# Three small attentions in a transformer stack: two tiles side by side in rounds, or one tile after the other on every engine

## The reference, cut to what matters

```python
x = x + _L0_attn_ref(_layernorm(x, axis=-1), ...)
Q = (X @ Wq.T + bq).reshape(B, S, H, d_head) * scale      # H = 16 heads of 16
K = (X @ Wk.T + bk).reshape(B, S, H, d_head) * scale
V = (X @ Wv.T + bv).reshape(B, S, H, d_head)
scores = jnp.einsum('bqhd,bkhd->bhqk', Q, K)              # causal mask, then softmax
out = jnp.einsum('bhqk,bhkd->bqhd', attn, V).reshape(B, S, D)
return out @ Wo.T + bo
```

## Time and profile before

| | |
|---|---|
| median of 3 runs | 3392.66 us (3380.62 to 3396.48) |
| the profiled execution's own time | 3396.48 us |
| its span in the profile | 3394.7 us |
| attention 1, in the span | 18.2 to 223.1 us |
| attention 2 | 229.8 to 441.5 us |
| attention 3 | 2537.4 to 2742.0 us |
| mean granted clock of TensorE | 0.928 of full speed |

### The profile page before, as it was taken

One profiled execution on the slowest core, in us unless ns is written; L12 is line 12 of the kernel. 1 busy time (PEld: TensorE's weight loads), 2 busy tenths in 40 slices (PEclk: granted clock), 3 DMA queues, 4 the chain that ended last, 5 costly groups with the idle time before them and its releaser, 6 DMA issues. The chain is left out here.

```text
span 3394.7 us, 49700 instructions
## 1 busy us (share of the span) xinstructions
PE 2916.8 (86%) x17527; PEld 1787.8 (53%) x17528; DVE 1579.7 (47%) x2705; ACT 1260.5 (37%) x2514; POOL 1232.9 (36%) x656
## 2 busy tenths in 40 slices
PE   5867734659999999999999999999977789999998
PEld 3544422535545554555455554555434467777776
DVE  3444567533554455444544464445526643333232
ACT  3433412114344334433443344344424333333332
POOL 0000000035676567656765676557650000000000
PEclk9778866679999999999999999999988899999999
DMA  1000030011111011110111111111011000000000
GB/s 40 0 17 0 0 121 0 0 58 40 36 49 39 25 35 49 39 35 33 41 39 35 39 35 39 35 39 35 30 72 77 0 1 0 0 0 0 0 0 25
DMA packets 26434, 98.27 MB, mean 29 GB/s; under 512 B 3536, under 2 KB 8272, under 8 KB 24976
## 3 DMA queue, kind: packets, MB, share of 16 engines
q1 hardware_dynamic: 24720, 94.02, 8.4%
q10 hardware_dynamic: 1664, 3.58, 0.3%
HBM read 55.97 MB, written 2.10 MB: 17 GB/s over the span
## 5 line engine op out<-in xcount | busy, mean ns | idle before, releaser
L685 POOL TENSOR_TENSOR cx_acc<-cx_acc,cx_prob 128x1024 f32<-128x1024 f32 (+1 forms) x352 | 834.7, 2371 | 509.0 <-ACT cx_prob L965 501.5
L965 ACT ACTIVATE cx_prob<-cx_st 128x512 f32<-128x512 f32 (+1 forms) x832 | 477.5, 596 | 595.2 <-PE cx_st L814 577.5
L1062 DVE TENSOR_REDUCE cx_mhalf<-cx_mx 128x1 f32<-128x804 f32 x512 | 486.1, 988 | 219.2 <-PE cx_mx L790 219.1
L825 PE MATMUL cx_av<-cx_prob,cx_kv 128*64 128x512 f32 (+1 forms) x1664 | 456.8, 628 | 0.0
L813 PE MATMUL cx_st<-cx_q,cx_k 128*128 128x512 f32 (+1 forms) x832 | 369.0, 444 | 50.0 <-ACT cx_prob L965 49.4
L1528 PE MATMUL moe_gu<-moe_wgu,moe_xnT 128*128 128x352 f32 x1280 | 397.6, 462 | 0.0
L790 PE MATMUL cx_mx<-cx_kp,cx_q 128*128 128x402 f32 x1024 | 304.0, 380 | 62.6 <-DVE cx_mhalf L1062 59.2
L814 PE MATMUL cx_st<-cx_q,cx_k 128*128 128x512 f32 (+1 forms) x832 | 332.4, 400 | 0.0
L1528 PEld LDWEIGHTS moe_gu<-moe_wgu,moe_xnT 128*128 128x128 f32 x1280 | 241.5, 191 | 124.1 <-issue 6.2
L790 PEld LDWEIGHTS cx_mx<-cx_kp,cx_q 128*128 128x128 f32 x1024 | 174.7, 193 | 248.5 <-DVE cx_mhalf L1062 186.0
L1043 DVE TENSOR_TENSOR cx_turn<-cx_mx,cx_tab 128x384 f32<-128x384 f32 x256 | 130.9, 553 | 358.3 <-PE cx_mx L747 358.3
(11 more groups left out here) (209 smaller groups left out, 3701.3 us busy)
## 6 DMA issues: line engine op xcount, KB each, us to landing
cx_k<-cx_kp SPq DMA_DIRECT2D x32, 804.0 KB, 4.0
cx_ctx<-in_cx_ctxN SPq DMA_DIRECT2D x32, 416.0 KB, 3.2
cx_ctxr<-in_cx_ctxrN SPq DMA_DIRECT2D x32, 416.0 KB, 3.9
cx_k<-cx_kp SPq DMA_DIRECT2D x32, 402.0 KB, 5.2
moe_wgu<-in_moe_wgu SPq DMA_DIRECT2D x5, 1408.0 KB, 14.6
moe_wd<-in_moe_wd SPq DMA_DIRECT2D x4, 896.0 KB, 24.6
x_all<-in_x SPq DMA_DIRECT2D x1, 2048.0 KB, 4.2
cx_wq<-in_cx_wq SPq DMA_DIRECT2D x1, 2048.0 KB, 11.8
```

The source lines that it names most:

```text
L685: pool.tensor_tensor(acc[rows, :, :], sofar, prob[slot(kt)][rows, :, :], ALU.add).then_inc(s_acc, 1)
L825: last = pe.matmul(av[DCX * p:DCX * p + DCX, :], kv[e][0:nk(kt), kt, :], prob[slot(kt)][0:nk(kt), p, :], start=(kt == 0), stop=(kt == NKT ...
L965: act.activation(prob[slot(kt)][rows, p, :], st[p][rows, :], ACT.Exp).then_inc(s_exp, 1)
L1062: dve.tensor_reduce(mhalf[:, i // 2, i % 2:i % 2 + 1], mx[i % 2][:, :, 0:KQ], AX.XY, ALU.max)\
```

## The change

`rounds` goes out, for these three attentions, for `staggered`: the loop body treats one tile at a time, and each stage in it is given with the number of tiles by which it is ahead. `SLOTS`, the buffers and the six rounds in the loop (the last two are written out) stay at two tiles. In attentions 1 and 2 queries and keys are projected with the weights as the stationary side and `xnT` as the moving one, so that they come out transposed: `turn_qk`, `qk` and `keep_qk`'s old form go, and matmuls of 256 or 512 columns become twice or four times as many of 128. ScalarE adds the biases of attention 2 when it keeps `qT` and `kbd`. In all three, keys are transposed in `front`, not in `v`.

```diff
+def staggered(engine, first, body, start=lambda r: None):
+    def at(r, g, ahead):
+        return r + (g + ahead) // SLOTS, (g + ahead) % SLOTS
+    for stage, tile in first:
+        stage(*at(0, 0, tile))
+    with engine.Fori(0, ROUNDS - 2) as r:
+        start(r)
+        for g in range(SLOTS):
+            for stage, ahead in body:
+                stage(*at(r, g, ahead))
...
             def turn_x(r, g):
-                pe.wait_ge(s_xn, r * SLOTS + before + g + 1)
+                pe.wait_ge(s_xn, upto(r, g))
+                if not is_first(r):
+
+                    pe.wait_ge(s_kbd, upto(r - 1, g))
...
+                elif kind == "bias":
+                    for o in range(2 * DC):
+                        for c in range(DC):
+                            last = pe.matmul(front[g][:, o * P:(o + 1) * P], w["qk"][:, c, o * P:(o + 1) * P],
+                                             xnT[g][:, c, :], start=(c == 0), stop=(c == DC - 1))
...
             def scores(r, g):
 
-                pe.wait_ge(s_x, LEAD + r * SLOTS + before)
-                pe.wait_ge(s_qTc, r * SLOTS + before + g + 1)
-                pe.wait_ge(s_kbd, r * SLOTS + before + g + 1)
+                pe.wait_ge(s_x, two_before(r, g))
+                pe.wait_ge(s_kbd, upto(r, g))
...
-            rounds(pe, (turn_x, project, turn_qk),
-                   ((scores, 0), (turn_x, 1), (turn_probs, 0), (project, 1), (values, 0), (turn_qk, 1), (out, 0)))
+            if kind == "rope":
...
+                          ((turn_probs, 0), (turn_x, 3), (scores, 1), (values, 0), (turn_qk, 2), (project_qk, 3),
+                           (project_v, 2), (out, 0)))
+            else:
...
+                          ((turn_probs, 0), (turn_x, 2), (scores, 1), (values, 0), (project_qk, 2), (project_v, 2),
+                           (out, 0)))
...
+                    for c in range(DC):
+                        act.activation(qT[g][:, c, :], front[g][:, c * P:(c + 1) * P], ACT.Identity,
+                                       bias=w["bq"][:, c:c + 1])
+                    for c in range(DC):
+                        for i in range(4):
+                            last = act.activation(kbd[g][:, c, i, :], front[g][:, D + c * P:D + (c + 1) * P],
+                                                  ACT.Identity, bias=bk4[:, c, i:i + 1], scale=head4[:, i:i + 1])
...
+                staggered(act, ((keep_xT, 0), (keep_xT, 1), (keep_qk, 0), (keep_v, 0), (keep_qk, 1), (keep_v, 1),
+                                (exps, 0)),
+                          ((keep_probT, 0), (keep_xT, 2), (exps, 1), (keep_qk, 2), (keep_v, 2)))
...
+                          ((gather, 4), (shift, 1), (normalise, 4), (scale_heads, 0), (turn, 3), (update_x, 0)),
+                          start)
+            else:
...
+                          ((gather, 3), (shift, 1), (normalise, 3), (scale_heads, 0), (update_x, 0)),
+                          start)
```

More of the change, by code:

```diff
@@ L74, in rounds @@
                 stage(ROUNDS - 1, g)
+def staggered(engine, first, body, start=lambda r: None):
[8 more added lines that the diff above has]
+                stage(*at(r, g, ahead))
+    start(ROUNDS - 2)
+    for r in range(ROUNDS - 2, ROUNDS):
+        for g in range(SLOTS):
+            for stage, ahead in body:
+                if r * SLOTS + g + ahead < NT:
+                    stage(*at(r, g, ahead))
 def small_attention(nc, sb, pb, sem, kind, name, w, x_all, const, nth, steps_before):
@@ L143, in small_attention, with upto, two_before @@
     s_dve = sem("attention_dve_step")
-    steps_ahead = 2 + SLOTS * {"context": 0, "bias": 0, "rope": 1}[kind]
-    dve_steps = 2 + SLOTS * {"context": 2, "bias": 2, "rope": 3}[kind]
+    F = 3 if kind == "rope" else 2
+    tile_steps = 5 if kind == "rope" else 4
+    steps_ahead = 2 * (F + 1) + (F if kind == "rope" else 0) + 1
     def is_first(r):
         return isinstance(r, int) and r == 0
+    def upto(r, g):
+        return r * SLOTS + before + g + 1
+    def two_before(r, g):
+        return LEAD + r * SLOTS + before + g - 1
     with nc.Block() as block:
@@ L187, in turn_x, with project_qk @@
                 last.then_inc(s_xT, 1)
-            def project(r, g):
-                pe.wait_ge(s_xTc, r * SLOTS + before + g + 1)
-                if kind == "context":
-                    pe.wait_ge(s_ctx, r * SLOTS + before + g + 1)
-                    for c in range(DC):
-                        pe.matmul(front[g][:, 0:D], xnT[g][:, c, :], w["q"][:, c, :],
-                                  start=(c == 0), stop=(c == DC - 1))
-                    last = pe.matmul(front[g][:, D:2 * D], ctxT[g][:, :], w["k"][:, :], start=True, stop=True)
-                else:
+            def project_qk(r, g):
+                pe.wait_ge(s_xTc, upto(r, g))
+                if kind == "rope":
                     for c in range(DC):
@@ L253, in values @@
             def values(r, g):
-                pe.wait_ge(s_pTc, r * SLOTS + before + g + 1)
+                pe.wait_ge(s_pTc, upto(r, g))
                 for c in range(DC):
@@ L267, in out @@
             def out(r, g):
-                pe.wait_ge(s_on, r * SLOTS + before + g + 1)
+                pe.wait_ge(s_on, upto(r, g))
                 for c in range(DC):
@@ L351, in keep_qk, with gather @@
[L351 to L365 removed]
+            def gather(r, g):
+                x = x_all[:, bass.ds(r * SLOTS + g, 1), :]
+                step.done(dve.bn_stats(stats[g][:, :], x))
+                dve.memset(mv[0][:, 2:3], 0.0)
+                step.done(dve.bn_aggr(mv[g][:, 0:2], stats[g][:, :]))
+                dve.tensor_scalar(mv[g][:, 1:2], mv[g][:, 1:2], EPS, None, ALU.add).then_inc(s_var, 1)
@@ new lines, in normalise, with turn @@
+            def normalise(r, g):
+                x = x_all[:, bass.ds(r * SLOTS + g, 1), :]
+                dve.wait_ge(s_rstd, upto(r, g))
+                if not is_first(r):
+                    dve.wait_ge(s_xT, upto(r - 1, g))
+                dve.tensor_scalar(xn[g][:, :], x, mv[g][:, 0:1], rstd[g][:, 0:1], ALU.subtract, ALU.mult)\
+                    .then_inc(s_xn, 1)
+            def turn(r, g):
+                dve.wait_ge(s_qk, LEAD + upto(r, g))
+                t2p = t2[g][:, :].rearrange("p (n e) -> p n e", e=2)
+                fp = front[g][:, :].rearrange("p (n e) -> p n e", e=2)
+                sn = w["sin"][:, :].rearrange("p (n e) -> p n e", e=2)
+                dve.tensor_tensor(t1[g][:, :], front[g][:, :], w["cos"][:, :], ALU.mult)
+                dve.tensor_tensor(t2p[:, :, 0], fp[:, :, 1], sn[:, :, 0], ALU.mult)
+                step.done(dve.tensor_tensor(t2p[:, :, 1], fp[:, :, 0], sn[:, :, 1], ALU.mult))
+                dve.tensor_tensor(qk[g][:, :], t1[g][:, :], t2[g][:, :], ALU.add).then_inc(s_qkc, 1)
@@ L387, in start @@
             def start(r):
-                step.start(r * dve_steps + steps_before + steps_ahead)
+                step.start(r * SLOTS * tile_steps + steps_before + steps_ahead)
             step.start(steps_before)
-            rounds(dve, (normalise, keep_qk),
-                   ((normalise, 1), (shift, 0), (keep_qk, 1), (scale_heads, 0), (update_x, 0)), start)
-    return steps_before + ROUNDS * dve_steps
+            if kind == "rope":
+                staggered(dve, ((gather, 0), (gather, 1), (normalise, 0), (normalise, 1), (gather, 2), (normalise, 2),
+                                (turn, 0), (turn, 1), (turn, 2), (gather, 3), (normalise, 3), (shift, 0)),
+                          ((gather, 4), (shift, 1), (normalise, 4), (scale_heads, 0), (turn, 3), (update_x, 0)),
+                          start)
+            else:
+                staggered(dve, ((gather, 0), (gather, 1), (normalise, 0), (normalise, 1), (gather, 2), (normalise, 2),
+                                (shift, 0)),
+                          ((gather, 3), (shift, 1), (normalise, 3), (scale_heads, 0), (update_x, 0)),
+                          start)
+    return steps_before + NT * tile_steps
 CH, CK, CQ = 16, 128, 192
```

128 lines of the change are left out of this document (57 added, 71 removed).

## The result

The changed kernel takes 3291.05 us, the median of 4 runs (3290.18 to 3293.69); the kernel before, beside it, 3388.9 (4 runs, 3380.62 to 3396.48). The ratio is 0.9713, 95% interval 0.9687 to 0.9739: 2.9% faster, with the forecast of 3292 beside it. That agreement is partly luck: the total is right to 1 us, but between first and last scores one stage is 5.7 us worse than forecast and the two others together 7.2 us better. The profiled execution has a span of 3288.6 us, against 3394.7 for the one taken of the kernel before.

What follows compares the result with a forecast made beforehand. No engine was full: both tiles sat in softmax together, idling TensorE. Staggered steps of 8.9 to 9.2 us, with clock falls in attention 1, save about 105 us from 3396.48, giving 3292 us; range 3265 to 3345.

Steps and rivals of the forecast that it cites:

- The sum: Three attention stages take 148.3, 133.8 and 139.8 us, saving 104.4; with starts and tails about 105 us, giving 3292.
- The small terms: First scores about 3 us sooner in attention 1, 2 in attention 2, 3.7 later in 3; tails plus 0.3 each.
- a third tile's projection: Start of attention 3: a third tile is projected first, so the first scores come 3.7 us later.
- The cycle: VectorE's chain from `scores` to `scores`: 8.9 us a tile in attentions 1 and 2, 9.2 in 3, where `update_x` decides.
- my sum: TensorE's own work per tile in attention 2, from scores, transposes, values, projections and `out`: 7.6 us.
- the 4.8 of the range's end: Attention 2's 16 projection matmuls: 1.8 us, or 4.8 if new weights were not hidden behind a column stream.
- TensorE's 8.1 us in attention 3: TensorE's own work per tile in attention 3, which keeps `turn_qk` (four transposes, 0.46 us): 8.1 us.
- Rival C: All three attentions: gain lost in issue, six waits per tile costing 2.2 us a tile; 3392, chance 0.08 with what lies between.
- Rival D: All three attentions: slower, TensorE at 1.2 GHz with its work doubled to 13.9, 15.2 and 16.2 us; 3500, chance 0.05.
- hidden below 8.9 either way: ScalarE in attention 2: 6.0 us a tile, at most 8.2, covered because `values` can be 2 us late.
- The clock in attention 1: A 2.0 us wait for `out` drops TensorE's clock in about every second tile, making steps 9.9 us.
- Rival B: Clock swings in all three attentions from short waits, one fall of 2.0 us in every tile; 3357, chance 0.20.

Runs made afterwards that it cites:

- run 3: Changed kernel plus four more 128-column ScalarE activations a tile in attention 2 and one more VectorE rotation product in attention 3: 3320.34 us.
- run 9: Changed kernel with attention 1's context and its key and value weights padded with zeros from 64 to 128 rows: 3284.36 us.
- run 2: Changed kernel with attention 1's values made twice on TensorE and attention 2's `xn` made two more times on VectorE, into scratch: 3294.94 us.
- run 7: Changed kernel with `xn` made early, right behind its statistics and ahead of `shift`, in all three attentions: 3279.16 us.
- run 1: Changed kernel with `xn` made later, behind `scale_heads` in attentions 1 and 2 and behind `update_x` in attention 3: 3288.26 us.
- run 6: Changed kernel with attention 1's first 128 query columns projected twice and attention 2's query and key biases left out (five ScalarE instructions, not ten): 3285.15 us.
- run 10: Changed kernel with attention 1's context zero-padded, `xn` early in all three, and attention 2's key bias left out (four 256-column spreads): 3255.36 us.
- run 8: Kernel before with the stagger alone, queries and keys of attentions 1 and 2 still transposed, POOL's power ahead of the context copy: 3305.71 us against 3392.58.
- run 5: Kernel before, in rounds of two tiles, with only the turned projections of attentions 1 and 2 and biases on ScalarE: 3371.04 us against 3391.96.

## Why the prediction was right, and where it wasn't

**The sum.** Between first and last scores the three stages save 19.9, 47.7 and 38.1 us, 105.7 in all, where 104.4 was forecast. The first scores of attention 1 come 3.1 us sooner (forecast 3), those of attention 2 1.9 sooner counted from attention 1's last (forecast 2), those of attention 3 2.7 later (forecast 3.7), and what follows attention 3's last scores takes 2.0 us more. Together: 105.7 + 3.1 + 1.9 - 2.7 - 2.0 = 106.0; the two spans differ by 106.1. Each stage is within 6 us of its forecast: 154.0 for 148.3, 130.3 for 133.8, 136.1 for 139.8.

The small terms came out by luck. In run 3 attention 1 has the code of the changed kernel, and its first scores come at 27.4 us, not 30.3, because TensorE was at the lower clock for less of the start-up. The second tile's query matmuls, in the changed kernel and then in run 3:

```profile
26.14 2.07 PE L234 MATMUL a_front<-a_xnT,a_wq 128*128 128x128 f32 x8
...
25.06 1.16 PE L236 MATMUL a_front<-a_xnT,a_wq 128*128 128x128 f32 x8
```

In run 9, whose attention 2 has the changed kernel's code, its first scores come 40.0 us behind attention 1's last ones, where it was 38.5 and 40.4 before. And the way from attention 2's last scores to attention 3's first takes 2128.7 to 2135.7 us in the ten staggered kernels, so that its 2.7 us say little of a third tile's projection.

**The cycle: right.** 8.73 against 8.9 in attention 2 and 9.0 against 9.2 in attention 3. The waits for `out` were 1.72, 0.99 and 0.70 us against 2.0, 1.3 and 0.8, each a little shorter. In attention 2 TensorE's own work is 0.2 us longer than my sum: the 16 matmuls of the turned projection took 1.99 us (277.25 to 279.24) where I had 1.8, far from the 4.8 of the range's end. (TensorE's 8.1 us in attention 3 add up to 8.0 from my own terms; nothing hangs on it.) The stretches are 183, 164 and 171 us for 176, 166 and 174. The granted clock of "above 0.95" in attentions 2 and 3 was missed over the whole stretches (0.92 and 0.94) and met between first and last scores (0.99 and 0.97). The nature of the chain was tested from both sides: 0.65 us more on VectorE made attention 2 0.65 slower (run 2), one product more made attention 3 0.33 slower (run 3), and `xn` moved off the chain made attention 3 0.25 faster (run 7). Rival C is out, by attention 2 from its first to its last scores (busy time, then the waits):

```profile
222.90:353.20 130.30, 112.66 (x1597) 86.94 (x1596) 85.21 (x137) 92.86 (x237) 16.59 (x26) 0.99 0.00 1
```

```profile
PE a_score L303 <- DVE a_headsT L427: 13.6, 14, 1.0
```

Of 130.3 us TensorE is busy 112.7 and waits 13.6 for `headsT`; all else, issue included, is 4.0 us, 0.3 a tile. Rival D is out: in the steps of attention 1 TensorE at the lower clock got the full one back after 3.4 us each time.

**ScalarE: the step that failed, at no cost.** I said ScalarE is "hidden below 8.9 either way: what covers it is that `values` can be 2 us late". Two things are wrong in it. The ten activations of 128 columns take 3.4 us (279.82 to 283.21), not 2.9. And I compared ScalarE's busy time with the step (6.0 us forecast, 101.15 / 16 = 6.3 measured), and looked for slack only ahead of `values`, where ScalarE's chain does not end. It ends at the `scores` of the next tile: scores to `shift` (1.69 + 2.40 and 0.11 to the exponentials), those (0.97), `qT` and `kbd` (3.4), hand-over (0.17), together 8.73. That is a loop of its own, with ScalarE idle 2.40 us in it and yet no slack, and it came out as long as VectorE's chain. That the prediction did not suffer is luck. By run 3, where 1.37 us more of ScalarE's work cost 1.37 us a step, the upper end of my own range, 5.1 us for the ten, would have made attention 2 1.7 us a tile slower, about 25 us (an estimate), and I had called that free. Runs 1, 6 and 10 show that there are two loops. The Trainium skill, "ScalarE: Activation LUTs", section "What ACT_TABLE_LOAD costs", led to some 3.7 us for the ten, an estimate; the trace has 3.4, and my own figure was 2.9, so that of the Trainium skill was nearer.

**The clock in attention 1: the mechanism right, the size wrong.** I forecast a fall in "about every second tile" and 9.9 us a step; from the second step on it fell in every one, at 1.5 to 1.8 us each (steps of 10.24 to 10.57 less 8.73; forecast 2.0 with what it delays), 10.4 a step in the mean and the 5.7 us that the stage is over. The mis-sized term is thus the share of tiles: "every second" came from no row, and by my own reading a wait of 2.0 us, longer than the 1.81 that was not borne, had to fell the clock in every one. Rival B's mechanism thus ruled attention 1 and neither of the others.

The reading of the earlier trace rows failed as well: I took the length of the wait as the whole condition, with 1.66 us borne and 1.81 not. Where the matmuls around the wait use all rows of the array, that fits all that was measured: 1.67 us borne in every tile of attention 2 (run 2), 1.59 to 1.70 borne in attention 1 (run 10), 1.91 not (run 9). Where keys and values of a context of 64 stand ahead of the wait, on half of the rows, waits of 1.27 to 1.40 us were enough in most tiles (runs 1, 2, 6, 7, 8). The padded context turned 141.9 us into 126.7 (run 7 against 10), though the wait grew by 0.2 us. That pair shows that the padding keeps the clock at this wait. The padding puts zeros on the other 64 rows, and it also lets the projections pass 0.19 us sooner (run 9); which of the two the clock answers to, no run separates. That runs 1, 2, 6, 7 and 8 have both kinds of steps in one stage, behind waits of one length, suggests that the phase counts too; no run tests it.

The rule that I took from the Trainium skill, "TensorE: Matmul & The Clock Gate", section "A second HAM failure mode: psum-queue depth-cycling", on clock swings from short idles between groups of matmuls, agrees with attention 1 and not with 1.67 us in every tile of attention 2.

**The parts.** I gave the turned projection no term of its own for the order before. It is worth 21 us without the stagger, most of it by another phase of the clock (run 5). With the stagger it is worth 11 to 15, of which 8 are a shorter start-up of attention 2 and the rest is clock, part of it in other blocks (run 8). The steady step of attention 2 does not depend on it. The stagger makes up the rest.

## What to carry to other kernels

With engines in order, compute every loop that closes on itself, by the engine that closes it: an engine that is 70% busy can be the bound if what it waits for starts late in the step. If taking a suspected bound away gives nothing, look for a second loop of the same length before dropping the idea; here each alone gave nothing, and both 0.3 us a tile. An idle of TensorE costs more than itself once the clock falls behind it, so shorten it, or try padding half-used arrays with zeros when the columns are streamed anyway: here it kept the clock only once the wait was shorter too (run 10, not run 9).

## What the runs showed of the hardware that was not expected

- TensorE's clock fell behind waits of 1.27 to 1.40 us where 64-row matmuls stood ahead of them, and stayed up behind waits of 1.59 to 1.70 us in every tile where all 128 rows were in use; zeros in the added rows sufficed (granted clock of attention 1 0.97 instead of 0.88, runs 10 and 7).
- One fall of 3.4 us cost 1.5 to 1.8 us and came back with the tile: 14 falls 10.24 us apart in attention 1, with steps that shrank from 10.57 to 10.24 us.
- ScalarE's activations of 128 columns with a scale and a bias read from memory pass at 0.34 us each in a row (run 3); four of 256 columns with a scale alone passed at 0.36 each (420.02 to 421.46 in the kernel before, where the next operation starts). Eight thus cost nearly twice what four do (2.90 and 1.57 us). It is not that columns are free: the two of 128 columns for `qT`, with a bias alone, passed at 0.25 each (279.82 to 280.31). Half the columns saved 0.1 us, and the second operand read from memory cost it again.
